# The score masks of both attentions as 26 extra contraction rows of the diagonal fills

## The reference, cut to what matters

```python
# layer 0
qkv = jnp.einsum('bte,fe->btf', xn, in_proj_weight)        # heads of width 8
scores = jnp.einsum('bhqd,bhkd->bhqk', q / sqrt(8), k)
scores = jnp.where(pos[:, None] >= pos[None, :], scores, -inf)
x = x + softmax(scores) @ v @ Wout + fp4_ffn(xn)
# layer 1
kc = conv(xn, stride 3); k_tmp = concat([xn[:, :1], kc])   # 342 keys
mask = (k_idx[None, :] * 3.0 >= q_idx[:, None] + 0.001)
scores = q @ k.T * 8 ** -0.5 + mask * -1e9
x = x + softmax(scores) @ v @ Wo + bo + experts(xn)        # 8 experts, top 2, one shared
```

## Time and profile before

| what | value |
|---|---|
| device time, median of 3 runs | 1237.9 us (1234.62 to 1257.37) |
| the profiled execution, device time | 1236.83 us |
| its span, first to last instruction | 1234.9 us |
| granted TensorE clock, mean | 0.955 of full |
| PE / DVE / ACT / POOL busy | 91% / 76% / 60% / 36% |
| first block | up to about 80 us |
| fp4 feed-forward | 80 to 187 us |
| attention of layer 0 | 187 to 690 us |
| between the layers | 690 to 776 us |
| attention of layer 1 | 776 to 1000 us |
| experts | 1000 to 1235 us |

### The profile page before, as it was taken

One profiled execution on the slowest core, in us unless ns is written; L12 is line 12 of the kernel. 1 busy time (PEld: TensorE's weight loads), 2 busy tenths in 40 slices (PEclk: granted clock), 3 DMA queues, 4 the chain that ended last, 5 costly groups with the idle time before them and its releaser, 6 DMA issues. The chain is left out here.

```text
span 1234.9 us, 22211 instructions
## 1 busy us (share of the span) xinstructions
PE 1122.0 (91%) x7511; PEld 614.9 (50%) x7518; DVE 935.3 (76%) x2098; ACT 735.9 (60%) x1148; POOL 447.5 (36%) x714
## 2 busy tenths in 40 slices
PE   4668879999999999999998697799999989999997
PEld 2345663344444444343443374444444448888874
DVE  7979988688888888888884372877787636777776
ACT  3557640666666666666666453356666667787762
POOL 6002220142323332332222120387776622566630
PEclk9989996899999999999999897799999989999999
DMA  4322790003302130212000013222222253687542
GB/s 137 96 84 64 113 125 2 19 27 108 101 13 93 41 116 23 82 55 85 28 2 2 1 54 86 67 64 61 64 65 61 58 169 127 188 258 245 163 122 83
DMA packets 94975, 103.52 MB, mean 84 GB/s; under 512 B 17217, under 2 KB 72838, under 8 KB 94864
## 3 DMA queue, kind: packets, MB, share of 16 engines
q1 hardware_dynamic: 88928, 93.09, 28.0%
q0 software_dynamic: 4992, 8.48, 2.0%
q10 hardware_dynamic: 944, 0.54, 0.2%
HBM read 64.67 MB, written 38.43 MB: 83 GB/s over the span
## 5 line engine op out<-in xcount | busy, mean ns | idle before, releaser
L1136 ACT ACTIVATE a_probs<-a_pst 128x1024 f32<-128x1024 f32 (+4 forms) x544 | 413.9, 813 | 274.9 <-PE a_pst L1084 274.3
L1160 DVE TENSOR_REDUCE a_tops<-a_ps 128x1 f32<-128x512 f32 (+9 forms) x624 | 340.9, 589 | 84.4 <-PE a_ps L1054 76.6
L992 POOL TENSOR_SCALAR_AFFINE_SELECT a_probs<-a_probs 128x256 f32<-128x256 f32 (+3 forms) x384 | 180.6, 481 | 366.8 <-ACT a_probs L1136 361.4
L1054 PE MATMUL a_ps<-kp,qp 96*128 96x512 bf16 (+9 forms) x1280 | 293.5, 307 | 0.0
L1084 PE MATMUL a_pst<-qp,kp 99*128 99x512 bf16 (+4 forms) x1088 | 259.1, 330 | 15.2 <-DMA qp<-a_top_rows 11.5
L1103 PE MATMUL a_po<-a_probs,vh 128*32 128x512 f32 (+4 forms) x2176 | 232.0, 499 | 2.6 <-POOL a_probs L992 2.5
L1160 DVE TENSOR_REDUCE a_tops_lead<-a_ps 128x1 f32<-128x512 f32 x256 | 161.6, 681 | 5.9 <-PE a_ps L1054 5.6
L1054 PEld LDWEIGHTS a_ps<-kp,qp 96*128 96x128 bf16 x1280 | 111.4, 100 | 79.1 <-DVE a_tops_lead L1160 15.5
L1051 PE MATMUL a_ps<-mask_s,identb 128*128 128x128 bf16 (+8 forms) x624 | 144.1, 234 | 6.8 <-PEq L1254 4.4
L1084 PEld LDWEIGHTS a_pst<-qp,kp 99*128 99x128 bf16 (+1 forms) x1088 | 91.8, 99 | 110.9 <-ACT a_probs L1136 47.2
L1738 POOL DMA_INDIRECT chosen_rows<-e_slot_y,e_slot_x x92 | 93.3, 1014 | 97.0 <-DVE e_slot_y L1958 75.3
(11 more groups left out here) (314 smaller groups left out, 1624.0 us busy)
## 6 DMA issues: line engine op xcount, KB each, us to landing
e_slot_w<-weight_parts SPq DMA_DIRECT2D x23, 1024.0 KB
qp<-q_parts SPq DMA_DIRECT2D x64, 96.0 KB
slot_rows<-empty_row SPq DMA_DIRECT2D x4, 1495.0 KB, 27.2
e_slot_x<-slot_rows SPq DMA_DIRECT2D x23, 260.0 KB, 3.1
a_raw<-in_wraw SPq DMA_DIRECT2D x18, 256.0 KB, 3.6
weight_parts<-first_rows SPq DMA_DIRECT2D x9, 512.0 KB, 3.0
weight_parts<-a_cut SPq DMA_DIRECT2D x9, 512.0 KB, 3.1
qp<-q_parts SPq DMA_DIRECT2D x64, 64.0 KB
```

The lines of the kernel that those rows point to most:

```text
L992: pool.affine_select(out=seen, in_=seen, compare_op=ALU.is_ge, fill=0.0, base=m0, pattern=[[0, 2], [1, mw]], channel_multiplier=-1 if laye ...
L1054: last = pe.matmul(bank[:, i * room:i * room + w], sb["qp"][slot][0:KROWS, j, f["qt"] * P:(f["qt"] + 1) * P], sb["kp"][slot][0:KROWS, j // ...
L1136: act.activation(probs[local % RING][0:st["rows"], 2 * part:2 * part + 2, st["off"]:CHUNK], p_st[part][0:st["rows"], :, st["off"]:CHUNK], ...
L1160: dve.tensor_reduce(out, scores, AX.X, ALU.max).then_inc(s["banks_read"], 1)
```

## The change

- Rows 99 to 124 of `qp` and `kp` (`AFTER` = 26 rows, so `CROWS` = 125) hold powers of two, whose products add up to about zero where a key is seen and to a very negative number where it is not. Five keys share one row, at steps of 2^25.
- A diagonal fill no longer has a mask matmul. Each of its heads becomes two matmuls: the *plain* columns over 96 rows, and the diagonal columns over 125 rows. Where the whole width is diagonal there is only the second.
- The diagonal part also reads rows 96 to 98 of `qp`, so they have to be zero until the maxima are stored. After each `next_load` SP issues one more DMA that writes zeros (24 KB, from a DRAM tensor `no_maxima` that a new DMA fills in the feed-forward block). The wait for `loaded` counts it.
- POOL draws the rows. In the first block `draw_after` runs behind the last `root`: 2 memsets, 11 selects of 128x128, one memset of 3 rows, and 8 copies into `kp` (29 rows x 2048) and `qp` (29 rows x 4096). The four memsets of line 303 and the mask tiles with their selects go. For layer 1 the rows are drawn in `between_layers`: two `draw_after(t)` behind each of root(0) to root(3), each a memset, ten selects (128x43 and 128x128 in turn, a wait after each two) and one more select; and one `lay_after(g)` behind each of root(4) to root(7), with a copy of 29 x 684 and one of 29 x 4096.
- The planner's `fill_pe` is now the number of columns times `COLUMN_US` for all heads, without a mask and without the floor `LOAD_US`. The order it writes changes from there on.

```diff
-        fill_pe = [len(f["heads"]) * max(LOAD_US, f["width"] * COLUMN_US) + len(f["heads"]) * f["mask"][1] * COLUMN_US
-                   if f["mask"] else max(LOAD_US, f["width"] * COLUMN_US) for f in self.fills]
+        fill_pe = [len(f["heads"]) * f["width"] * COLUMN_US for f in self.fills]
...
+                    sp.dma_start(sb["qp"][n % GROUPS][KROWS:KROWS + PARTS, :, :].rearrange("r j t -> r (j t)").bitcast(F32),
+                                 dram["no_maxima"]).then_inc(sb["loaded"][n % GROUPS], 16)
...
-                if f["mask"]:
-
-                    r, mw = f["mask"]
-                    out = bank[:, :].rearrange("p (h k) -> p h k", h=nh)[:, :, w - mw:w]
-                    pe.matmul(out, sb["identb"][:, :], mask_s[r][:, 0:mw].unsqueeze(1).broadcast_to([P, nh, mw]),
-                              start=True, stop=False, skip_group_check=True)
+                plain = w - f["mask"][1] if f["mask"] else w
                 for i, j in enumerate(f["heads"]):
-                    last = pe.matmul(bank[:, i * room:i * room + w],
-                                     sb["qp"][slot][0:KROWS, j, f["qt"] * P:(f["qt"] + 1) * P],
-                                     sb["kp"][slot][0:KROWS, j // 2, f["k0"]:f["k0"] + w],
-                                     start=not f["mask"], stop=True, skip_group_check=True)
+                    for rows, at, to in ((KROWS, 0, plain), (CROWS, plain, w)):
+                        if at < to:
+                            last = pe.matmul(bank[:, i * room + at:i * room + to],
+                                             sb["qp"][slot][0:rows, j, f["qt"] * P:(f["qt"] + 1) * P],
+                                             sb["kp"][slot][0:rows, j // 2, f["k0"] + at:f["k0"] + to],
+                                             start=True, stop=True, skip_group_check=True)
...
+            def draw_after():
+                row0 = KROWS + PARTS
+                pool.memset(after_k[:, :], 0.0).then_inc(drawn, 1)
+                pool.memset(after_q[:, :], -2.0 ** (EQUAL - KEY0 + JUMP)).then_inc(drawn, 1)
...
+                for d in range(STEP):
+                    pool.affine_select(out=after_k[:, :], in_=after_k[:, :], compare_op=ALU.not_equal,
+                                       fill=2.0 ** (KEY0 + JUMP * d), base=STEP * row0 - d, pattern=[[1, P]],
+                                       channel_multiplier=-STEP).then_inc(drawn, 1)
...
+                for g in range(GROUPS):
+                    for rows, after in ((sb["kp"][g], after_k), (sb["qp"][g], after_q)):
+                        wide = rows[KROWS:CROWS, :, :].rearrange("r j (t n) -> r (j t) n", n=P)
+                        pool.tensor_copy(wide, after[KROWS:CROWS, :].unsqueeze(1).broadcast_to(list(wide.shape)))\
+                            .then_inc(drawn, 1)
...
+            for n in range(CHUNKS):
+                if n > CHUNKS // 2:
+                    pool.wait_ge(drawn, 2 + DRAWS * BT + 2 * (n - CHUNKS // 2))
+                root(n)
+                if n < CHUNKS // 2:
+                    draw_after(2 * n)
+                    draw_after(2 * n + 1)
...
+                if n >= CHUNKS // 2:
+                    lay_after(n - CHUNKS // 2)
```

More of the change, by code:

```diff
@@ L94 @@
 ROW = E + 2
+NONE = 64
 NOWHERE = 1 << 24
@@ L300, in _ @@
             pool.wait_ge(shaped, SQUARE)
[L301 to L309, removed]
+            for b in range(2):
+                root(b)
+                pool.wait_ge(root_steps, 2 * b + 2)
             pool.memset(sb["earlier"][:, :], 1.0).then_inc(built, 1)
@@ L319, in _ @@
             pool.wait_ge(built, BUILT)
[L321 to L327, removed]
             for n in range(2):
@@ L876, in attention @@
     v_all = sb[f"v{layer}"]
-    mask_s = [sb["mask_s0"][:, :]] if layer == 0 else [sb["mask_s1"][:, r, :] for r in range(STRIDE)]
     with ExitStack() as ctx:
@@ L943, in _ @@
                 sp.wait_ge(sb["counts"]["between"]["k_stored"], START + STORES * B)
+            if layer == 0:
+                sp.wait_ge(sb["later_in"], 16 * (sb["later_loads"] + 5))
             use = 0
@@ L1291, in _, with root @@
         def _(pool):
-            for n in range(CHUNKS):
+            def root(n):
                 pool.wait_ge(s["moment_steps"], START + 6 * (n + 1))
@@ L1297, in _, with draw_after @@
                     .then_inc(s["root_steps"], 1)
+            DRAWS = 2 * STEP + 2
+            def draw_after(t):
+                row0, rest, base = KROWS + PARTS + t % 2 * SET, P * t % STRIDE, 1 + DRAWS * t
+                first, last = P * t // STRIDE, (P * t + P - 1) // STRIDE + 1
+                ks, qs = after_k[:, first:last], after_q[:, t * P:(t + 1) * P]
+                pool.memset(qs, -2.0 ** (EQUAL - KEY0 + JUMP)).then_inc(drawn, 1)
+                for d in range(STEP):
+                    pool.wait_ge(drawn, base + 1 + 2 * d)
+                    pool.affine_select(out=ks, in_=ks, compare_op=ALU.not_equal, fill=2.0 ** (KEY0 + JUMP * d),
+                                       base=STEP * row0 - d, pattern=[[1, last - first]], channel_multiplier=-STEP)\
+                        .then_inc(drawn, 1)
+                    pool.affine_select(out=qs, in_=qs, compare_op=ALU.is_ge,
+                                       fill=-2.0 ** (EQUAL - KEY0 - JUMP * d) if d < STEP - 1 else 0.0,
+                                       base=STRIDE * (d - STEP * row0) - rest - 1, pattern=[[-1, P]],
+                                       channel_multiplier=STRIDE * STEP).then_inc(drawn, 1)
+                pool.wait_ge(drawn, base + 1 + 2 * STEP)
+                pool.affine_select(out=qs, in_=qs, compare_op=ALU.is_ge, fill=0.0, base=row0 + SET - 1, pattern=[[0, P]],
+                                   channel_multiplier=-1).then_inc(drawn, 1)
@@ new lines, in lay_after @@
+            def lay_after(g):
+                for rows, after in ((sb["kp"][g][KROWS:CROWS, :, 0:KEYS1], after_k), (sb["qp"][g][KROWS:CROWS, :, :], after_q)):
+                    pool.tensor_copy(rows, after[KROWS:CROWS, :].unsqueeze(1).broadcast_to(list(rows.shape)))\
+                        .then_inc(drawn, 1)
+            pool.memset(after_k[:, :], 0.0).then_inc(drawn, 1)
+            for n in range(CHUNKS):
[6 more added lines that the diff above has]
+                if n >= CHUNKS // 2:
+                    pool.wait_ge(s["root_steps"], START + 2 * n + 2)
+                if n == CHUNKS // 2:
+                    pool.wait_ge(drawn, 1 + DRAWS * BT)
+                    pool.memset(after_k[KROWS:KROWS + PARTS, :], 1.0).then_inc(drawn, 1)
+                    pool.wait_ge(drawn, 2 + DRAWS * BT)
+                if n >= CHUNKS // 2:
+                    lay_after(n - CHUNKS // 2)
```

36 lines of the change are left out of this document (28 added, 8 removed).

## The result

The changed kernel takes 1345.4 us (median; 1343.2 to 1347.7) against 1238.0 us for the kernel before on the same chip: a ratio of 1.087, 95% interval 1.084 to 1.090. It is slower, by some 107 us, and far outside the forecast range. The profiled execution of after has a span of 1342.2 us against 1234.9.

What follows compares the result with a forecast made beforehand. PE was taken to bound both attentions and DVE the first block; -15 - 9.5 + 20 + 8 = +3.5 us on the profiled 1236.8 gave 1240 us, range 1216 to 1264.

Steps and rivals of the forecast that it cites:

- Attention of layer 0, masks: Attention of layer 0: removing the masks takes 26 us off PE; net -15 us after what comes back.
- 6 for the order: Attention of layer 0: less PE work between `turn_max` and the first pair in every second unit; +6 us.
- 5 for DVE: Attention of layer 0: DVE at 83% busy, with three banks between it and PE, gives back +5 us.
- the dearer price: Attention of layer 0: the skill's 81 ns per 128-column matmul, instead of 57, would make the sum 10 us higher.
- Attention of layer 1: Attention of layer 1: 7.5 us of masks off PE, some 5 recovered, 3 for bank waits; net -9.5 us.
- The extra DMAs themselves: Attentions: 24 DMAs of 24 KB on SP, behind 12 loads each, cost 0.
- should recover some 5 of the 7.5 us: Attention of layer 1: more work behind `turn_max` regains some 5 us of PE's 7.5 us wait for the maxima's DMA.
- The first block: First block: POOL's eight copies hold DVE's instructions, one getting through per copy; +20 us in sum.
- The first rival: First block: POOL's copies leave DVE alone, so the block costs nothing; 1220 us, chance 0.15.
- Between the layers: Between the layers: POOL's draws put root after root at 8.0 us, copies add nothing; +8 us.
- The slowest of them: POOL's copies run at the two-input pace: first block +45, three `lay_after` 5 us each; 1280 us, chance 0.06.
- The third: Layer 0's attention: DVE and the maxima's round trip take over, only 5 of 26 us arrive; 1250 us, chance 0.17.

Runs made afterwards that it cites:

- the old order: The changed kernel with the planner's cost of a diagonal fill put back as before, so its order of steps too; 1267.7 us, ratio 1.026.
- The fastest kernel: Changed kernel with planner's order undone, STORE_US 3.4, second next_load held on SP, draws in attention 0, first copies on ScalarE in feed-forward; 1213.4 us, ratio 0.980.

## Why the prediction was wrong

- **Attention of layer 0, masks: right in size, wrong in what came back.** Predicted 26 us off PE, then 6 for the order and 5 for DVE: -15; measured +11. The columns left as said: in the steady window PE's column time fell by 25 us, and its busy time in the old order by 21 (465.2 to 444.6). The extra pieces took 57 ns each, as the prediction had taken from the earlier trace rows against the dearer price that it names beside it. The new order cost 20 us (after against the old order), not 6. The term that failed is the planner's order: I had weighed the work behind `turn_max` in one unit, and neither PE's waits for VectorE that another order brings (6.3 us instead of 1.9) nor the clock, which fell behind them and cost 13 us. Why the new order's steps fit the three banks worse was not taken further. And with the old order a wait that the prediction did not price appeared: the masks had themselves been cover for the maxima's way, 4.0 us of waiting became 12.4.
- **Attention of layer 1: the failed step that decides.** Predicted -9.5, measured +61. The sentence "SP is not what any engine waits for there except for the maxima ...: 0" names the very exception. It costed the new DMAs as one landing, and did not go through SP's program in the new order, in which 13 + 13 issues of 0.7 us stand ahead of a maxima's store. The trace of the kernel before held both numbers: 12 loads at 0.6 to 0.8 us of issue each, and a way of 3.4 us with no slack left, as PE already waited 0.26 us at its end. Nor did I look where the new order put `next_load`, only where it put fills and pairs; "should recover some 5 of the 7.5 us" had the sign wrong.
- **The extra DMAs themselves: right.** The fastest kernel issues all of them, and its attention 1 takes 218.4 us.
- **The first block: right.** Predicted +20, measured +18. The copies took 2.2 and 3.9 us in that stretch, with one DVE instruction each. The sum had given the eight copies 23.3 us and DVE's turns 4.0 more; they ran back to back and were through in 23.8:

```profile
53.34 3.79 POOL L320 COPY qp<-n_after_q 29x4096 bf16<-29x4096 bf16 x1
53.71 3.71 DVE L146 TENSOR_SCALAR n_m<-n_m 128x512 f32<-128x512 f32 x1
57.08 2.09 POOL L320 COPY kp<-n_after_k 29x2048 bf16<-29x2048 bf16 x1
57.45 2.25 DVE L148 TENSOR_TENSOR n_v<-n_v,n_m 128x512 f32<-128x512 f32 x1
...
65.41 4.06 POOL L320 COPY qp<-n_after_q 29x4096 bf16<-29x4096 bf16 x1
65.93 4.38 DVE L380 TENSOR_SCALAR n_xn<-x,mean,rstd 128x128 f32<-128x128 f32 x4
...
73.41 0.69 DVE L148 TENSOR_TENSOR n_v<-n_v,n_m 128x512 f32<-128x512 f32 x1
```

  Line 148 takes 0.69 us when POOL is idle and 2.25 when it copies. The first rival, that copies leave DVE alone, is out.
- **Between the layers: right mechanism, wrong size.** Predicted +8, measured +16. A draw took 3.73 us, not 3.05, and root followed root after 8.7 us, not 8.0:

```profile
729.66 0.20 POOL L1317 TENSOR_SCALAR b_var<-b_var 128x4 f32<-128x4 f32 x1 [5.58 <-DVE b_var L168]
...
730.92 0.20 POOL L1329 MEMSET b_after_q<- 128x128 bf16 x1
...
734.65 0.20 POOL L1329 MEMSET b_after_q<- 128x128 bf16 x1
...
738.34 0.19 POOL L1317 TENSOR_SCALAR b_var<-b_var 128x4 f32<-128x4 f32 x1
```

  That is 2.8 us more for root(4) than the forecast had, of the 4 that are missing to the 12 us of the draws; for the rest I have no row. The copies, which I had put at nothing, cost 4, because they hold the normalisation that the next chunk needs, as in the first block (4.85 us for its four instructions beside a copy, 1.11 with none):

```profile
765.98 4.85 DVE L1591 TENSOR_SCALAR rows<-x,mean,rstd 128x128 f32<-128x128 f32 x4 [1.76 <-POOL rstd L1319]
766.45 0.75 POOL L1346 COPY kp<-b_after_k 29x684 bf16<-29x684 bf16 x1
767.15 3.60 POOL L1346 COPY qp<-b_after_q 29x4096 bf16<-29x4096 bf16 x1
...
788.70 1.11 DVE L1591 TENSOR_SCALAR rows<-x,mean,rstd 128x128 f32<-128x128 f32 x4
```

  I had the mechanism in the part on the first block and did not carry it over.
- **The rest:** 0, and measured 0 to 1.

None of the rivals was the cause of the slowdown: all of them dealt with engines, none with SP's queue. The slowest of them ended at 1280. The third named a part that came true once the order was undone: the maxima's round trip took over in layer 0, and only 8 of the 26 us arrived.

## What to carry to other kernels

An edit of a cost in a planner is not bookkeeping: print the orders it makes, old and new, and go through every engine's program in them, the DMA issuer's too. Count what is issued ahead of each short transfer that an engine waits for, and price it at the issue time per DMA. Work that leaves the bounding engine was perhaps the cover of a round trip; before counting it as gained, ask what the engine will do until the round trip ends.

## What the runs showed of the hardware

- A GpSimd copy held one VectorE instruction for as long as it ran (3.79 us beside 3.71, 2.09 beside 2.25), also a TENSOR_SCALAR with per-partition scalars: the four of line 380 at 65.93 took 4.38 us, and those of the kernel with the copies on ScalarE 0.34 us each. The prediction had said of this line (360 in the kernel before) that it never waited; the first block of that kernel has no such copy. The Trainium skill (SBUF — State Buffer, section "SBUF: two separate sides") speaks of an exclusive lock on ports that the two engines share, held for a whole instruction; the rows from 53.34 on agree.
- A copy from SBUF to SBUF over 29 rows moved at 16 GB/s, with a DMA share of 0.08 of the 16 engines; cut into 3 and 26 rows, at 95 GB/s with 0.43, and attention 0 began 2 instead of 77 us behind the stage before. The Trainium skill (DMA: Bandwidth & Descriptors, section "Why a DMA increments its semaphore by 16 and not by 1") says that a DMA goes to the largest number of engines, up to 16, that divides the slowest dimension of both its sides. An estimate by that rule is 1 engine for 29 rows, 13 for 26 and 3 for 3. The two runs agree with it in kind: the shares are 1.3 and 6.9 engines.
- The granted clock of TensorE fell where it waited: 0.87 in attention 1 with the waits of 8 us, 0.96 with the same instructions and without them, and the matmuls were busy for 14 us less. In attention 0 of after it fell to the lower level five times behind waits of 0.2 to 1.1 us that followed each other.
